# One of the 16 score tiles of an image moves from VectorE to ScalarE and TensorE's quarter sums, and the low halves accumulate onto the product that is already in PSUM

## What is computed

```
v = (x @ wqv_w.T + wqv_b).reshape(b, t, 3 * h, d)
q, vf, vb = (v[:, :, :h], v[:, :, h:2 * h], v[:, :, 2 * h:])
k = x[:, :, None, :] * wk[None, None]
a[b, s, t, h] = -sum_w |q[b, s, h, w] - k[b, t, h, w]| / sqrt(64)
a = softmax(a with a row of zeros appended, axis=1)[:, :t]
bf = einsum('bsdh,bshw->bdhw', a, vf);  bb = einsum('bdsh,bshw->bdhw', a, vb)
o = (bf + bb).sum(axis=2)
y = o * sigmoid(1.702 * o) @ fanin_w.T + fanin_b;  return x + y
```

## Time and profile before

| | |
|---|---|
| median of 3 runs | 2579.14 us (2575.05 to 2579.5) |
| profiled execution | 2576.05 us, of which the span is 2574.2 us |
| L1 attention | first tile at 720.5 us, last pair's first tile at 2438.7 us: 63 pairs in 1718 us |
| one pair in the steady loop | about 27.2 us |
| mean granted TensorE clock | 0.962 |

### The profile page before, as it was taken

The page is one execution under the profiler, slowest core; times in us unless marked ns, Lnnn a source line. Parts: engine busy times, 40 slices in busy tenths (PEclk is TensorE's granted clock), DMA queues, the critical chain, the costliest instruction groups (busy, mean ns, idle before and its releaser), DMA issues.

```text
span 2574.2 us, 45353 instructions
## 1 busy us (share of the span) xinstructions
PE 2236.6 (87%) x12251; PEld 961.1 (37%) x12251; DVE 2244.8 (87%) x2638; ACT 1475.2 (57%) x3772; POOL 1767.2 (69%) x1033
## 2 busy tenths in 40 slices
PE   5558999999388989989989989899899899899878
PEld 3443333333123333333333333333333333333347
DVE  3877777777879999999999999999999999999974
ACT  0325555555146666666666666666666666666656
POOL 0112333333459889888888988888898888889843
PEclk8788999999689999999999999999999999999979
DMA  5200000000012112121211221221221212212201
GB/s 132 65 1 1 1 0 0 0 0 0 3 47 52 48 48 52 48 50 49 51 48 48 52 50 45 51 51 45 50 52 48 50 48 50 50 47 52 50 19 32
DMA packets 163216, 102.06 MB, mean 40 GB/s; under 512 B 55773, under 2 KB 161182, under 8 KB 163039
## 3 DMA queue, kind: packets, MB, share of 16 engines
q1 hardware_dynamic: 162858, 101.41, 16.0%
q10 hardware_dynamic: 316, 0.12, 0.0%
HBM read 10.63 MB, written 4.19 MB: 6 GB/s over the span
## 4 chain that ended last, share of the span: by engine, by line
PE 65%; DVE 23%; issue 9%; ACT 1%; DMA 1%; DVEq 0%; SPq 0%; POOL 0%; ACTq 0%; POOLq 0%
DVE score L1454 17%; PE pp L802 16%; PE pp L796 7%; PE pp L636 5%; PE pp L767 3%; PE pp L657 3%; PE pp L723 3%; PE pp L715 2%; PE pp L661 2%; PE pp L731 2%; PE pp L711 2%; PE pp L721 2%; PE pp L658 2%; PE pp L662 2%; PE pp L628 2%
## 5 line engine op out<-in xcount | busy, mean ns | idle before, releaser
L1454 DVE TENSOR_REDUCE score<-pp 128x16 f32<-128x1024 f32 x1408 | 1647.0, 1219 | 101.9 <-PE pp L802 82.2
L1571 POOL TENSOR_TENSOR absd<-absd 128x2560 f32<-128x2560 f32 x635 | 1442.4, 2271 | 197.1 <-ACT absd L1074 157.2
L802 PE MATMUL pp<-blocks,pick 128*128 128x512 f16 x2816 | 817.0, 383 | 155.0 <-DVE score L1454 150.4
L1074 ACT ACTIVATE absd<-pp 128x512 f32<-128x512 f32 x1280 | 695.4, 598 | 368.0 <-PE pp L796 364.1
L802 PEld LDWEIGHTS pp<-blocks,pick 128*128 128x128 f16 x2816 | 211.2, 98 | 590.7 <-DVE score L1454 421.9
L796 PE MATMUL pp<-blocks,pick 128*128 128x512 f16 x1280 | 400.0, 383 | 2.1
L1538 POOL TENSOR_TENSOR absd<-absd,yw 128x512 f32<-128x512 f32 x112 | 142.1, 1269 | 318.8 <-DVE yw L1376 318.8
L1008 ACT ACTIVATE absd<-pp 128x512 f32<-128x512 f32 x256 | 150.7, 596 | 148.1 <-PE pp L658 146.6
L1392 DVE SCALAR_TENSOR_TENSOR absd<-pp,absd 128x512 f32<-128x512 f32 x256 | 172.5, 688 | 52.9 <-ACT absd L1008 38.4
L796 PEld LDWEIGHTS pp<-blocks,pick 128*128 128x128 f16 x1280 | 119.8, 97 | 248.3 <-ACT absd L1074 84.6
L1056 ACT CAST qk<-pp 128x512 f16<-128x512 f32 x130 | 76.0, 585 | 191.2 <-PE pp L724 191.2
(11 more groups left out here) (227 smaller groups left out, 2497.9 us busy)
## 6 DMA issues: line engine op xcount, KB each, us to landing
blocks<-qk SPq DMA_DIRECT2D x1032, 64.0 KB, 2.0
attn<-score SPq DMA_DIRECT2D x1024, 16.0 KB, 1.8
xs<-xn SPq DMA_DIRECT2D x66, 32.0 KB, 1.8
big<-in_wrb_t SPq DMA_DIRECT2D x1, 2064.0 KB
big<-in_x_rows SPq DMA_DIRECT2D x4, 512.0 KB, 6.1
token_rows<-big SPq DMA_DIRECT2D x8, 256.0 KB, 2.0
big<-in_L_ffn_w SPq DMA_DIRECT2D x4, 512.0 KB, 10.1
out<-h SPq DMA_DIRECT2D x16, 128.0 KB, 2.0
```

Source lines behind the costliest of these rows:

```text
L802: mm = pe.matmul(ps[bank + n], pick[:, unit % 8 + n, :], blocks[:, b, unit // 16, unit // 8 % 2, :], start=True, stop=True)
L1074: nc.scalar.activation(absd[odd][:, 16 * u + 8 * n:16 * u + 8 * n + 8, :], ps[4 + n].rearrange("p (h w) -> p h w", w=D), ACT.Abs).then_inc ...
L1454: dve.tensor_reduce(score[:, odd, b, 16 * d:16 * d + 16], pp[:, bank:bank + 2, :].rearrange("p n (h w) -> p (n h) w", w=D), AX.X, ALU.add, ...
L1571: nc.gpsimd.tensor_tensor(x[:, :, 0:w], x[:, :, 0:w], x[:, :, w:2 * w], ALU.add).then_inc(X["tree"], 1)
```

## The change

1. ORDER becomes `DADDADDADDADADED`: 10 D tiles, 5 A tiles, and one "E" tile at k=14 that was D. D tiles always alternate the two pairs of banks from the pair's first.
2. The E tile is laid out the other way round (`blocks` is the weights, `pick` moves, four matmuls of 256 columns), so that its 64 summands lie on partitions. ScalarE writes the absolute values to `abse`, a part of the `absd` buffers that the tree doesn't read. GpSimd now waits for the A tiles alone.
3. A pair later, behind tile k=11 of image 0 of pair q, `sum_e(q-1)` adds both images' E tiles by 8 f32 matmuls with `pair_ones` (32 columns of weights each, 256 moving columns). ScalarE copies the 128 x 256 result (`copy_e`), `turn_e(q-1)` behind k=13 turns it with two f32 matmuls of 16 columns, and ScalarE writes it into `score` (`take_e`, which counts `etaken`).
4. `spread(p, ...)` on SP also waits for `etaken` of its pair.
5. `low` no longer repeats the product: the f16 matmul accumulates onto what lies in bank 6.
6. The exponentials of a pair go in four groups of two heads rather than two of four, the first group behind tile k=7 of image 1 rather than k=10; turn_attn goes from k=4 to k=5, the gate of the output on VectorE from reduce 8 to 7.
7. One more small constant is loaded, `c_cols` lies in `absd0`, and a few small memsets are added, all ahead of the loop.

```
-ORDER = "DADDADDADDADDADD"
+ORDER = "DADDADDADDADADED"
...
+                sp.wait_ge(X["etaken"], p + 1)
...
             def low(p, odd, kind):
                 pe.wait_ge(X["half"], 4 * p + 2 * kind + 1)
-                if kind:
-                    pe.matmul(ps[6], xT1[:, odd, :], wk_diag[:].rearrange("p h d -> p (h d)"), start=True, stop=False)
-                else:
-                    pe.matmul(ps[6], xTq[:], wqv[:, 0:QK], start=True, stop=False)
-                pe.matmul(ps[6], neg_eye[:], qk[:, kind, 0, :], start=False, stop=True)...
+                pe.matmul(ps[6], neg_eye[:], qk[:, kind, 0, :], start=False, stop=True, skip_group_check=True)...
...
+            def sum_e(p, first):
+                pe.wait_ge(X["abs"], 4 * NA * (p + 1))
+                if not first:
+                    pe.wait_ge(X["etaken"], p)
+                for m in range(4):
+                    for b in range(2):
+                        mm = pe.matmul(ps[7][32 * m:32 * m + 32, 0:2 * P], pair_ones[:, b, :], abse[b][:, m, :],
+                                       start=(b == 0), stop=(b == 1))
+                mm.then_inc(X["e_ps"], 1)
+            def turn_e(p):
+                pe.wait_ge(X["esum"], p + 1)
+                for g in range(2):
+                    mm = pe.matmul(ps[7][:, 256 + 16 * g:272 + 16 * g], esum[:, P * g:P * g + P], row_of[:], start=True, stop=True)
+                mm.then_inc(X["et_ps"], 1)
...
+                                for m in range(2):
+                                    mm = pe.matmul(ps[4 + n][:, 256 * m:256 * m + 256],
+                                                   blocks[:, b, 1, 1, P * (2 * n + m):P * (2 * n + m) + P],
+                                                   pick[:, 6:8, :].rearrange("p a b -> p (a b)"), start=True, stop=True)
...
                         if k == 10:
                             queries(q + 1, at)
+                        if k == 11 and at >= 1:
+                            sum_e(q - 1, at == 1)
+                        if k == 13 and at >= 1:
+                            turn_e(q - 1)
...
+            def copy_e(p):
+                act.wait_ge(X["e_ps"], p + 1)
+                act.wait_ge(X["et_ps"], p)
+                nc.scalar.copy(esum[:], ps[7][:, 0:2 * P]).then_inc(X["esum"], 1)
+            def take_e(p, odd, at):
+                act.wait_ge(X["et_ps"], p + 1)
...
+                nc.scalar.copy(score[:, odd, :, 240:256].rearrange("p b (g h) -> p g b h", g=2),
+                               ps[7][:, 256:288].rearrange("p (g b h) -> p g b h", g=2, b=2)).then_inc(X["etaken"], 1)
...
                 absolute(s, 0, 3, q, first)
                 high_q(q + 1, False)
+                if at >= 1:
+                    copy_e(q - 1)
+                absolute(s, 0, 4, q, first)
                 low(q + 1, 0)
-                absolute(s, 0, 4, first)
+                if at >= 1:
+                    take_e(q - 1, 1 - odd, at - 1)
+                absolute(s, 0, 5, q, first)
```

More of the change, by code:

```diff
@@ L32 @@
 G8 = PAIRS // 8
-ORDER = "DADDADDADDADDADD"
-ND, NA = ORDER.count("D"), ORDER.count("A")
+ORDER = "DADDADDADDADADED"
+ND, NP = ORDER.count("D"), ORDER.count("A")
+NA = NP + 1
 W_SCALE = 64.0
@@ L97, in constants @@
         both[1, e, e // 2, e % 2] = 1.0 / LO_SCALE
+    row_of = np.zeros((4, 32, 2, 4, 2))
+    for m in range(4):
+        for b in range(2):
+            for a in range(2):
+                row_of[m, 2 * b + a, b, m, a] = 1.0
     same_head = np.kron(np.eye(16), np.ones((8, 8)))
@@ L852, in _ @@
             fan_in(last - 2)
+            pe.wait_ge(X["sum"], last - 1)
+            sum_e(last, False)
+            turn_e(last)
+            pe.wait_ge(X["etaken"], PAIRS)
             def last_turn(p):
@@ L1073, in absolute @@
                         act.wait_ge(X["pooled"], s - 1)
-                    nc.scalar.activation(absd[odd][:, 16 * u + 8 * n:16 * u + 8 * n + 8, :],
-                                         ps[4 + n].rearrange("p (h w) -> p h w", w=D), ACT.Abs).then_inc(X["abs"], 1)
+                    if u == NP and n == 0 and not first:
+                        act.wait_ge(X["e_ps"], q)
+                    if u < NP:
+                        nc.scalar.activation(absd[odd][:, 16 * u + 8 * n:16 * u + 8 * n + 8, :],
+                                             ps[4 + n].rearrange("p (h w) -> p h w", w=D), ACT.Abs).then_inc(X["abs"], 1)
+                    else:
+                        nc.scalar.activation(abse[odd][:, 2 * n:2 * n + 2, :].rearrange("p m n -> p (m n)"), ps[4 + n],
+                                             ACT.Abs).then_inc(X["abs"], 1)
+            def copy_e(p):
[4 more added lines that the diff above has]
+                act.wait_ge(X["et_ps"], p + 1)
+                if at >= 2:
+                    for b in range(2):
+                        act.wait_ge(X[f"spread{b}"], 16 * 8 * (p - 1))
+                nc.scalar.copy(score[:, odd, :, 240:256].rearrange("p b (g h) -> p g b h", g=2),
+                               ps[7][:, 256:288].rearrange("p (g b h) -> p g b h", g=2, b=2)).then_inc(X["etaken"], 1)
             def exponentials(p, part, first):
@@ L1084, in exponentials @@
                         act.wait_ge(X["zr"], p)
-                for n in range(4 * part, 4 * part + 4):
+                for n in range(2 * part, 2 * part + 2):
                     op = nc.scalar.activation(expd[:, n, :], attn[:, :, n], ACT.Exp, scale=-(float(D) ** -0.5),
                                               accum_out=zst[:, 0, n:n + 1])
-                if part:
+                if part == 3:
                     op.then_inc(X["exp"], 1)
@@ L1105, in pair @@
                 s, first = 2 * q, at == 0
-                absolute(s, 0, 0, first)
+                absolute(s, 0, 0, q, first)
                 if at >= 1:
@@ L1122, in pair @@
                 low(q + 1, 1)
-                absolute(s, 1, 0, first)
-                absolute(s, 1, 1, first)
+                absolute(s, 1, 0, q, first)
+                absolute(s, 1, 1, q, first)
                 if at >= 2:
                     turned_attn(q - 2)
-                absolute(s, 1, 2, first)
-                absolute(s, 1, 3, first)
+                absolute(s, 1, 2, q, first)
+                if at >= 1:
+                    exponentials(q - 1, 0, at == 1)
+                absolute(s, 1, 3, q, first)
                 if at >= 2:
@@ L1131, in pair @@
                 if at >= 1:
-                    exponentials(q - 1, 0, at == 1)
-                absolute(s, 1, 4, first)
+                    exponentials(q - 1, 1, at == 1)
+                absolute(s, 1, 4, q, first)
                 if at >= 1:
-                    exponentials(q - 1, 1, at == 1)
+                    exponentials(q - 1, 2, at == 1)
+                absolute(s, 1, 5, q, first)
+                if at >= 1:
+                    exponentials(q - 1, 3, at == 1)
             act.wait_ge(pads, PADS)
@@ L1151, in _ @@
             values_f(last, 1)
+            copy_e(last)
+            take_e(last, 1, 4)
             def root(c):
@@ L1175, in _ @@
             turned_y(last - 1)
-            exponentials(last, 0, False)
-            exponentials(last, 1, False)
+            for part in range(4):
+                exponentials(last, part, False)
             root(0)
@@ L1206, in _ @@
                 dve.memset(t, 0.0).then_inc(pads, 1)
-            dve.wait_ge(pads, 14)
+            dve.wait_ge(pads, 15)
             for t in (xT4[D:D + 1, :], xT1[D:D + 1], xTq[D:D + 1, :], yT[D:D + 1, :], xT5[D:D + 1]):
                 dve.memset(t, 1.0).then_inc(pads, 1)
+            for half in range(2):
+                at = slice(64 * half, 64 * half + 64)
+                for b in range(2):
+                    dve.memset(pair_ones[at, b, 2 * b + half:2 * b + half + 1], 1.0)
             dve.memset(wk_bd[:], 0.0)
@@ L1468, in pair @@
                             finish(q - 3, slot)
[L1469 removed]
+                        if b == 1 and d == 7 and at >= 2:
                             gated(q - 2)
@@ L1482, in _ @@
             dve.wait_ge(X["pooled"], 2 * last + 1)
-            dve.wait_ge(X["abs"], 2 * NA * (2 * last + 2))
-            dve.tensor_reduce(score[:, 1, 1, 16 * ND:256], absd[1], AX.X, ALU.add).then_inc(X["pooled"], 1)
+            dve.wait_ge(X["abs"], 2 * NA * (2 * last + 1) + 2 * NP)
+            dve.tensor_reduce(score[:, 1, 1, 16 * ND:16 * ND + 16 * NP], absd[1], AX.X, ALU.add).then_inc(X["pooled"], 1)
             def add_output(g):
```

53 lines of the change are left out of this document (34 added, 19 removed).

## The result

The changed kernel takes 2797.68 us (median of 4 runs, 2796.52 to 2799.37), the kernel before 2579.14. The ratio is 1.085, 95% interval 1.083 to 1.087. I had forecast 2960 us and slower, with a range of 2815 to 3040.

What follows compares the result with a forecast made beforehand. VectorE bounds the kernel before; the new SP wait closes a loop of 14.3 + 1.9 (clock) + 17.1 = 33.3 us against 27.2. 2576 + 378 for 62 steps + 5 at the end = 2960 us, range 2815 to 3040.

Steps and rivals of the forecast that it cites:

- VectorE and SP's slack: VectorE bounds the 27.2 us pair, 25.5 us busy; SP's queue of copies has 4.1 us to spare.
- The loop: First tile to take_e 14.3 us, then SP's copies to the next first tile 17.1: 31.4 us at full clock.
- Its second half: From take_e, 16 score copies and eight of blocks on SP, with semaphore and landing: 17.1 us.
- The term that failed first: sum_e on TensorE: 2.8 us, bounds 2.0 and 3.4; rival of quarters side by side 0.85 us, 2841 us total, chance 0.13.
- The row of values_f: Nearest TensorE row for pricing sum_e: four f32 matmuls of 256 columns in 1.01 us, read as five steps of 0.21.
- The term that failed second: Almost every pair begins at 1.2 GHz after TensorE's thin ending, costing 1.9 us, between 1.2 and 2.3.
- a case of a gap: Trace from 1670.6 to 1674.0, TensorE busy 1.81 of 3.40 us, then clock 0.50; cited as evidence for slow pair starts.
- the wait for VectorE at tile 9: 0.35 us TensorE wait for VectorE's backlog before the tile behind queries, taken as gone: 9.04 became 8.69 us.
- both failures as rivals: Clock holds, chance 0.13, and quarters of sum_e side by side, chance 0.13; each a 31.4 us loop and 2841 us.
- its likeliest part: Likeliest case alone: sum_e 2.0 to 3.4 and clock 1.2 to 2.3 us give 2865 to 3020 us; chance 0.60.
- The exponentials' chain: ScalarE's exponentials wait for the last score copy, until 25.7 us; last D tile ends near 30.1, below 31.4, no bound.
- Faster: Rival: take_e by 10 us, SP's slack hides the wait, TensorE's burst gives 25.6 us a pair, 2477 us; chance 0.04.

Runs made afterwards that it cites:

- e1: Changed kernel, take_e writing to a spare tile and SP's score copies not waiting for it, E tiles' scores left zero: 2543.17 us, 0.987 of the kernel before.
- e2: Changed kernel with the eight score copies of D-tile columns sent first, not waiting for take_e; output complete: 2541.21 us, 0.986 of the kernel before.
- e11: Changed kernel with the quarter sums of sum_e written to two row places (two column groups) in turn: 2823.48 us, 1.095 of the kernel before.
- e5: Changed kernel with all four quarter sums of sum_e written to rows 0 to 31 (one column group): 3008.13 us, 1.167 of the kernel before.
- e6: Changed kernel plus 15 idle f16 matmuls of 512 columns in the thin end of each pair: 2752.93 us, 1.068 of the kernel before.
- e8: e2 with ScalarE's exponentials regrouped, none between the last A tiles and the E tile: 2526.92 us, 0.980 of the kernel before.
- e9: e8 with keys one tile later and low of k behind tile 2 of image 1: 2462.07 us, 0.955 of the kernel before.
- e10: e2 with the repeated f32 products of low put back: 2592.13 us, 1.005 of the kernel before.

## Why the prediction was wrong in size and right in mechanism

*VectorE and SP's slack.* Right. VectorE lost the reduces and the pair gained nothing by it, and the 4.1 us of air in SP's queue were the number that mattered.

*The loop.* Right, and shown: with the wait gone (e1) or with eight copies moved ahead of it (e2) the slowdown is gone; a delay put ahead of take_e comes out in the pair (e11: 0.85 in, 0.82 out; e5: 2.56 in, and the rest of its 4.1 is the clock). Its second half, 24 issues and a landing, was priced at 17.1 us from the end of take_e. It measured 17.3 as the median in each of the changed kernel, e5, e11 and e6, while take_e's end moved from 12.7 to 16.8 us.

*The term that failed first: sum_e.* I took 2.8 us with a lower bound of 2.0; it measured 1.02. The 1.8 us too much are 110 us of the total. The row of values_f, 1.01 us for four f32 matmuls, had two readings. I took it for five steps of 0.21 in the order of the program, where only a direct neighbour on other rows overlaps. It is as well two column groups that each work off 4 records of 0.213 (0.85 us), side by side, plus 0.16. By the second reading sum_e is 0.85 + 0.16 = 1.0, whatever stands next to what in the program. e5, e11 and the changed kernel are one, two and four groups: 3.58, 1.87 and 1.02 us, which only the second fits. The trace before could have told: taken one by one rather than merged, the eight records of the values_f of the earlier trace rows start two by two, 0.01 us apart, at 1623.97, 1624.23, 1624.45 and 1624.67. The Trainium skill, page TensorE: Matmul & The Clock Gate, Part 3, said that column groups run concurrently; I quoted it, gave it 0.13, and the measurement agrees with it.

*The term that failed second: the clock.* I took 1.9 us for nearly every pair. The price was about right: the pairs with a slow start are 1.7 us longer than the others (31.78 against 30.05); the 1.2 to 1.5 of e6's expectation are too low. What failed is "almost every pair": only 28 of 62 have one, which is 0.75 us on average (e6). The 1.15 us too much are 71 us of the total. The same thin stretch at the end of a pair brings the clock down in one pair and not in the next. The trace before showed that too. The stretch of the earlier trace rows stands at the end of the pair before as well:

```profile
1643.60:1646.70 3.10, 1.60 (x6) 0.32 (x5) 3.10 (x5) 3.10 (x18) 1.79 (x4) 1.00 0.00 0
```

The pair behind it began at 1.00, and only 4 of the 62 steps before have a slow start (28.86 us rather than 27.19). The prediction calls the stretch from 1670.6 to 1674.0 a case of a gap, but it holds no long one: TensorE worked 1.81 us in it, and its longest pause was 0.66 us. What decides which pairs begin slow stays open.

*The sum.* Pair at full clock: 31.4 forecast, less 1.8 for sum_e, plus 0.34 for the wait for VectorE at tile 9 that I had struck out and that stayed, is 29.94; measured 30.05. The clock adds 0.75 rather than 1.9. 33.3 - 1.8 + 0.34 - 1.15 = 30.7 against a measured 30.8. The difference to 33.3, times 62, is the 160 us that were too much.

*The range.* I had both failures as rivals, each alone, both at 2841 us, and never put them together: with both, the same sum gives 62 x 2.3 + 5 + 2576 = 2724 us, and with half of the clock's 1.9 us left 2783. The range stopped at 2815, just below either case alone, and its likeliest part went by a lower bound of 2.0 us for sum_e from one reading of a row.

*What was rightly left out.* The exponentials' chain was at 30.1 against 31.4 in the prediction. In the trace the last tile of image 1 starts at 1670.11 and the next pair at 1672.26, so it was no bound. "Faster" needed take_e by 10 us; it came at 12.8.

## What to carry to other kernels

A new wait in a queue of DMA issues is priced by what stands behind it, not by how long it waits: take the time at which the wait is met, add every issue behind it and the landing, and compare that with when the last of them is needed. Copies that don't need the new result go ahead of the wait; that alone turned 1.085 into 0.986. When a row has two readings that price a new operation differently, both go into the range, and rivals that can both be true are also priced together. A price read at one place of a trace is multiplied only after counting at how many places it is paid.

## What the runs showed of the hardware that was not expected

- Eight f32 matmuls of 256 columns with 32 columns of weights take 3.58 us on one column group, 1.87 on two and 1.02 on four, although in the program two on the same group follow each other. The records on different groups start 0.01 to 0.03 us apart (changed kernel, e11). So here groups worked off their matmuls side by side, and so they did in values_f, where the program alternates the groups.
- 15 matmuls that nobody reads, in a stretch where TensorE was thinly used, took 45 us off the kernel, by keeping the granted clock at 1.00 where 28 of 62 pairs had begun at 0.50 (e6).
- How many of the 62 pairs begin slow differs from run to run in a way that the runs don't settle: 4 in the kernel before (27.3 us for a pair), 28 in the changed kernel (30.8), 9 in e11 (31.2), 59 in e5 (34.1), none in e1, e2, e8, e9 and e10 (25.5 to 27.5).
